# W2 loaded first and stored by rank, three casts ahead of the gelu layer, two low parts on GpSimd

## What is computed

```
ae = layernorm(cond) * ln_g + ln_b            # 2 x 256
h  = gelu(ae @ w1 + b1)                       # 2 x 256
xw = h @ w2 + b2                              # 2 x 4096, w2 is 256 x 4096
x_a, x_b = split(xw);  both reshape(2, 256, RANK=8)
layer = base_layer + einsum('bdr,bkr->bdk', x_a, x_b)
x = x + (x + x @ layer)
h_t = tanh(h_(t-1) @ Wh + x_t @ Wx + b)       # 1024 steps, h_0 = cond
out = x + h_t
```

## Time and profile before

| | us |
|---|---|
| median of 3 runs | 768.34 (767.2 to 768.7) |
| the profiled execution's own time | 767.74 |
| its span, from the first to the last instruction | 764.9 |
| the prologue, up to the first step of the recurrence | 30.25 |
| the recurrence and the last rows | the rest |

### The profile page before, as it was taken

One profiled execution on the slowest core, in us unless ns is written; L12 is line 12 of the kernel. 1 busy time (PEld: TensorE's weight loads), 2 busy tenths in 40 slices (PEclk: granted clock), 3 DMA queues, 4 the chain that ended last, 5 costly groups with the idle time before them and its releaser, 6 DMA issues.

```text
span 764.9 us, 45957 instructions
## 1 busy us (share of the span) xinstructions
PE 689.3 (90%) x18801; PEld 623.6 (82%) x18801; DVE 283.4 (37%) x1539; ACT 497.8 (65%) x5140; POOL 6.4 (1%) x18
## 2 busy tenths in 40 slices
PE   5699999999999999999999999999999999999997
PEld 5588888888888888888888888888888888888886
DVE  6533333333333333333333333333333333333332
ACT  6466666666666666666666666666666666666665
POOL 3000000000000000000000000000000000000000
DMA  8000000000000000000000000000000000000000
GB/s 279 10 6 10 11 11 9 11 7 9 11 11 8 11 8 9 11 11 9 10 7 9 11 11 9 11 7 9 11 11 9 11 8 7 11 11 9 7 7 6
DMA packets 12285, 12.36 MB, mean 16 GB/s; under 512 B 1813, under 2 KB 11056, under 8 KB 12080
## 3 DMA queue, kind: packets, MB, share of 16 engines
q1 hardware_dynamic: 11984, 9.45, 4.3%
q0 software_dynamic: 96, 0.02, 0.0%
HBM read 7.36 MB, written 2.10 MB: 12 GB/s over the span
## 4 chain that ended last, share of the span: by engine, by line
PE 76%; ACT 19%; issue 2%; DMA 1%; SPq 1%; DVE 1%; DVEq 0%; another core or an unknown queue 0%
PE acc L320 49%; ACT h_pre L446 19%; PE pre L320 14%; PE p_w L284 4%; PE pre L300 4%; PE p_w L279 2%; DMA x_in<-x_dram 1%; PE p_w L274 1%; PE pre L297 1%; SPq L218 1%; PE pre L401 0%; SPq L215 0%; DVE lay_s L687 0%; DVE lay_f L683 0%; DVE ab_t L676 0%
## 5 line engine op out<-in xcount | busy, mean ns | idle before, releaser
L320 PE MATMUL acc<-h_pre,wh_s 128*128 128x2 f16 x8192 | 385.5, 168 | 57.8 <-DVE acc L562 0.6
L446 ACT ACTIVATE h_pre<-pre 128x2 f16<-128x2 f32 x2046 | 240.7, 170 | 251.1 <-PE pre L320 251.1
L320 PEld LDWEIGHTS acc<-h_pre,wh_s 128*128 128x128 f16 x8192 | 302.2, 106 | 121.1 <-ACT h_pre L446 105.0
L567 DVE TENSOR_TENSOR h_lo<-p_f,h_pre 128x4 f16<-128x4 f32 x1024 | 165.5, 162 | 461.7 <-ACT p_f L452 457.1
L320 PE MATMUL pre<-h_rnd,wh_s 128*128 128x2 f16 x4092 | 270.2, 170 | 0.0
L320 PE MATMUL acc<-h_lo,wh_s 128*128 128x2 f16 x4096 | 257.5, 167 | 0.0
L320 PEld LDWEIGHTS pre<-h_rnd,wh_s 128*128 128x128 f16 x4092 | 190.7, 108 | 0.1
L320 PEld LDWEIGHTS acc<-h_lo,wh_s 128*128 128x128 f16 x4096 | 189.2, 106 | 0.1
L456 ACT ACTIVATE h_f<-acc 128x4 f32<-128x4 f32 x1024 | 186.4, 182 | 0.5 <-PE acc L320 0.5
L454 ACT ACTIVATE h_rnd<-acc 128x4 f16<-128x4 f32 x1022 | 172.7, 169 | 0.0
L452 ACT ACTIVATE p_f<-acc 128x4 f32<-128x4 f32 x1023 | 161.6, 158 | 0.1
(11 more groups left out here) (76 smaller groups left out, 139.4 us busy)
## 6 DMA issues: line engine op xcount, KB each, us to landing
w_f<-w_dram SPq DMA_DIRECT2D x8, 512.0 KB, 8.4
x_in<-x_dram SPq DMA_DIRECT2D x32, 64.0 KB, 2.3
out_dram<-o_row SPq DMA_DIRECT2D x64, 32.0 KB, 1.9
w_f<-w_dram SPq DMA_DIRECT2D x1, 256.0 KB, 2.8
base_f<-base_dram SPq DMA_DIRECT2D x1, 256.0 KB, 10.8
wh_f<-wh_dram SPq DMA_DIRECT2D x1, 256.0 KB, 10.5
wx_f<-wx_dram SPq DMA_DIRECT2D x1, 256.0 KB, 10.5
cond_r<-cond_dram SPq DMA_DIRECT2D x1, 2.0 KB
```

Of the source, the lines that this page charges most:

```text
L320: return nc.tensor.matmul(dst, wh_s[:, pw, ki, mo * P:(mo + 1) * P], h[:, par, ki, :], start=False, stop=True, skip_group_check=True)
L446: nc.scalar.activation(h_pre[:, n % 2, m, :], src, func, scale=scale).then_inc(s_hpre[(n // HALF) % 2], 1)
L567: nc.vector.tensor_sub(h_lo[:, par].rearrange("p m b -> p (m b)"), p_f[:, 0:COLS], h_pre[:, par].rearrange("p m b -> p (m b)")).then_inc(s ...
```

## The change

**The DMA queues.** SyncE issues piece 0 first, then W1, piece 1, the first block of `x`, pieces 2 to 7, `base`, `wh` and `wx`. The four small loads, `cond` and three vectors, move to ScalarE's queue, ahead of its first instruction.

```diff
-        w2_s = sb("w2_s", [P, 2, NM, 2 * D * RANK], F16)
+        w2_s = sb("w2_s", [P, 2, NM, 4, RANK, P], F16)
+        AHEAD = 3
+        POOLED = [3, 5]
+
+        def by_rank(ap):
+            return ap.rearrange("p (d r) -> p r d", r=RANK)
@@ gpsimd
+            for n in POOLED:
+                q, k = W2_PIECES[n]
+                pool.wait_ge(s_w2hi, n + 1)
+                nc.gpsimd.tensor_sub(w2_s[:, 1, k, q], by_rank(w2_f[:, k, tile_of_ab(q)]),
+                                     w2_s[:, 0, k, q]).then_inc(s_w2pool, 1)
@@ tensor
-            for n, (q, k) in enumerate(W2_PIECES):
+            for n in range(len(W2_PIECES)):
                 if n == 6:
                     turn_x()
...
+                pe.wait_ge(s_w2hi, n + 1)
+                w2_products(n, 0)
+                if n not in POOLED:
+                    pe.wait_ge(s_w2lo, n + 1 - len([m for m in POOLED if m < n]))
+                    last = w2_products(n, 1)
+                for m in POOLED:
+                    if n == m + 2:
+                        pe.wait_ge(s_w2pool, POOLED.index(m) + 1)
+                        last = w2_products(m, 1)
@@ scalar
+            def w2_high(n):
+                q, k = W2_PIECES[n]
+                act.wait_ge(s_w2[n], 16)
+                nc.scalar.copy(w2_s[:, 0, k, q], by_rank(w2_f[:, k, tile_of_ab(q)])).then_inc(s_w2hi, 1)
```

More of the change, by code:

```diff
@@ L140, in cond_recurrence @@
         s_w2lo = sem("s_w2lo")
+        s_w2pool = sem("s_w2pool")
         s_abcol = sem("s_abcol")
@@ L211, in _, with load_w2 @@
         def _(sync):
-            sync.dma_start(cond_r[:, :], cond).then_inc(s_cond, 16)
-            for n, v in enumerate((ln_g, ln_b, b1)):
-                sync.dma_start(vec_r[n * NM:(n + 1) * NM, :], v.rearrange("(m p) -> m p", p=P)).then_inc(s_vec, 16)
+            def load_w2(n):
+                q, k = W2_PIECES[n]
+                sync.dma_start(w2_f[:, k, tile_of_ab(q)], w2[k * P:(k + 1) * P, tile_of_ab(q)]).then_inc(s_w2[n], 16)
+            load_w2(0)
             sync.dma_start(w1_f[:, :, :], w1.rearrange("(k p) n -> p k n", p=P)).then_inc(s_w1, 16)
-            for n, (q, k) in enumerate(W2_PIECES):
-                sync.dma_start(w2_f[:, k, tile_of_ab(q)], w2[k * P:(k + 1) * P, tile_of_ab(q)]).then_inc(s_w2[n], 16)
+            load_w2(1)
+            sync.dma_start(x_in[:, :], x_rows[0:BLOCK]).then_inc(s_xload, 16)
+            for n in range(2, len(W2_PIECES)):
+                load_w2(n)
             sync.dma_start(base_f[:, :, :], base.rearrange("(k p) n -> p k n", p=P)).then_inc(s_base, 16)
-            sync.dma_start(x_in[:, :], x_rows[0:BLOCK]).then_inc(s_xload, 16)
             sync.dma_start(wh_f[:, :, :], wh.rearrange("(k p) n -> p k n", p=P)).then_inc(s_wh, 16)
@@ L392, in _, with w2_products @@
             pe.wait_ge(s_hid, 1)
-            for n, (q, k) in enumerate(W2_PIECES):
+            def w2_products(n, pw):
+                q, k = W2_PIECES[n]
+                for r in range(RANK):
+                    c = 64 + (q * RANK + r) * 2 * NB
+                    product = nc.tensor.matmul(pre[B][:, 0, c:c + 2 * NB], w2_s[:, pw, k, q, r, :],
+                                               hid_s[:, k].rearrange("p s b -> p (s b)"),
+                                               start=n == 0 and pw == 0 and r == 0, stop=True, skip_group_check=True)
+                return product
+            for n in range(len(W2_PIECES)):
                 if n == 6:
                     turn_x()
[L396 to L403, removed]
+                pe.wait_ge(s_w2hi, n + 1)
[7 more added lines that the diff above has]
+                        last = w2_products(m, 1)
             last.then_inc(s_abcol, 1)
@@ L471, in half_block @@
                         act.sem_clear(s_sum[1 - half])
+            act.dma_start(cond_r[:, :], cond).then_inc(s_cond, 16)
+            for n, v in enumerate((ln_g, ln_b, b1)):
+                act.dma_start(vec_r[n * NM:(n + 1) * NM, :], v.rearrange("(m p) -> m p", p=P)).then_inc(s_vec, 16)
             act.wait_ge(s_var, 1)
@@ L476, in _ @@
             nc.scalar.activation(warm[:, :], veps[:, :], ACT.Gelu)
+            def w2_high(n):
+                q, k = W2_PIECES[n]
+                act.wait_ge(s_w2[n], 16)
+                nc.scalar.copy(w2_s[:, 0, k, q], by_rank(w2_f[:, k, tile_of_ab(q)])).then_inc(s_w2hi, 1)
+            for n in range(AHEAD):
+                w2_high(n)
             act.wait_ge(s_hmm, 1)
@@ L488, in high @@
                                      scale=SCALE).then_inc(s_hi, 1)
-            for n, (q, k) in enumerate(W2_PIECES):
-                act.wait_ge(s_w2[n], 16)
-                nc.scalar.copy(w2_s[:, 0, k, tile_of_ab(q)], w2_f[:, k, tile_of_ab(q)]).then_inc(s_w2hi, 1)
+            for n in range(AHEAD, len(W2_PIECES)):
+                w2_high(n)
             high(wh_s, wh_f, s_wh)
@@ L636, in _, with w2_low @@
             last.then_inc(s_ae, 1)
+            def w2_low(n):
+                q, k = W2_PIECES[n]
+                dve.wait_ge(s_w2hi, n + 1)
+                nc.vector.tensor_sub(w2_s[:, 1, k, q], by_rank(w2_f[:, k, tile_of_ab(q)]),
+                                     w2_s[:, 0, k, q]).then_inc(s_w2lo, 1)
+            for n in range(AHEAD):
+                w2_low(n)
             dve.wait_ge(s_hidhi, 1)
             nc.vector.tensor_sub(hid_s[:, :, 1, :], hid[:, :, :], hid_s[:, :, 0, :]).then_inc(s_hid, 1)
[L641 to L650, removed]
+            for n in range(AHEAD, len(W2_PIECES)):
+                if n not in POOLED:
+                    w2_low(n)
             keep_x()
             split_x_high()
-            split_x_low()
             dve.wait_ge(s_b2, 16)
@@ L673, in _, with low @@
             last.then_inc(s_abst, 1)
+            def low(dst, src, n):
+                dve.wait_ge(s_hi, n + 1)
+                nc.vector.scalar_tensor_tensor(
+                    dst[:, 1].rearrange("p k n -> p (k n)"), src[:, :, :].rearrange("p k n -> p (k n)"), SCALE,
+                    dst[:, 0].rearrange("p k n -> p (k n)"), ALU.mult, ALU.subtract).then_inc(s_split, 1)
+            split_x_low()
             low(wh_s, wh_f, 0)
```

## The result

| | before | after |
|---|---|---|
| median | 768.37 us (767.2 to 768.7, 6 runs) | 773.87 us (773.31 to 774.93, 6 runs) |
| span of the profiled execution | 764.9 | 771.4 |
| VectorE's sum of the parts starts | 20.71 | 27.07 |
| first step of the recurrence | 30.25 | 36.61 |

A forecast was written before the change was run, and what follows sets the result against it. Only the recurrence's start could move: earlier loads and slower subtractions put the sum at 19.9 instead of 20.71, less 0.1 us for the new order, so 0.7 us earlier, 767.6 us; range 766.6 to 771.5.

The forecast's parts named there:

- What bounds the kernel: The recurrence has nearly all the time and stays unchanged; only its start, behind VectorE's sum, can move.
- The loads: W2's load stream on SyncE starts 1.30 us earlier; piece 7 lands at 16.05 instead of about 17.15.
- ScalarE's small loads: Four loads issued on ScalarE move its first table load from 0.74 to 2.04, the square root from 2.97 to 3.33.
- The cover: Gelu waits for the cast of piece 2, so up to 3.2 us of lateness on the conditioning path costs nothing.
- The hidden layer: TensorE's first W2 product moves from 9.21 to about 12.6; 128 products then take 4.2 us instead of 7.7.
- The step that failed: ScalarE's cast of W2 with a 32-byte read step was put at 1.05 us, between ends of 1.05 and 1.72.
- the first rival: ScalarE's casts slow too, to 1.72 us; the recurrence starts 2.4 us later, total 770.9 us; chance 0.22.
- The lock: GpSimd's and VectorE's subtractions keep each other out; the recurrence starts 2.7 us later, total 771.0 us; chance 0.18.
- two slow rivals: Slower ScalarE casts, 770.9 us, chance 0.22; GpSimd and VectorE keeping each other out, 771.0 us, chance 0.18.
- GpSimd's price: GpSimd's subtraction of 1024 elements takes at most 2.6 us; slowed by the step to 4.7, total 770.2, chance 0.05.

The follow-up runs named there:

- the step alone: Kernel before with only W2 stored by rank, so casts and subtractions read with a step of 32 bytes: 773.36 us, ratio 1.0073.

## Why the prediction was wrong

**What bounds the kernel** held. All of the difference arose ahead of the sum of the parts, and from the sum on both kernels need the same 9.54 us, where I had added 0.1 us for the new order.

**The loads** were right in kind and uncertain in size. Piece 0 landed at 4.9 (I said 4.7). The last piece landed near 16.2 in the changed kernel, near 15.9 in one run and 17.1 to 17.2 in others of the same order, where I had one figure, 16.05. Alone the part was worth 0.65 us, with an interval that includes no change, because VectorE was on the path. I had read its six low parts before as back to back; they lay (7.70 - 1.225) / 5 = 1.30 us apart, the pace of the loads, where one takes 1.225.

**ScalarE's small loads.** Its issues cost 1.45 us where I had 1.3; the square root ran at 3.73, between my 3.33 and 4.9. That the vectors would land at 5.6 I had missed: I priced the issue and not the transfer among 4 KB packets. The cover that I named, the cast of piece 2, did hide it in the changed kernel; with the loads alone there is no such cover, and it is on the path.

**The hidden layer** came later as I said, at 14.2 instead of 12.6 because the third cast took 2.03 us and the third subtraction 1.99. The loads by rank were as fast as forecast and TensorE kept up.

**The step that failed** is the choice of the cast at the low end, 1.05 us. It took 2.03, even above my upper end of 1.72. I had three rows and drew the wrong thing from each. TensorE's weight load, the only one that read SBUF, I turned into a rate that ScalarE would stay below, 2.1 elements per ns, while a cast whose every element leaves its 16 bytes took ScalarE 1.77 ns per element, more than twice its contiguous 0.82. Its factor of 1.8 I carried as a factor, though the faster engine loses more: 2.2 on ScalarE's slope, 1.7 on VectorE's. And the PSUM row, which holds for PSUM, says nothing of SBUF. The subtraction, put at 1.66 between 1.23 and 2.1, took 1.99. With 2.03 and 1.99 in my own sum for the first rival, the last cast ends near 22.4 and the sum starts near 25.2, which is close to the run without GpSimd (25.73).

**The lock** I held for possible with 0.18 and for the only cause in its case. It is real, and it came on top: 1.3 us from 25.73 to 27.07, and 2.05 us between the last cast and its subtraction. My two slow rivals were priced one at a time, while nothing made them exclude each other; both together lie beyond the range. The range itself left out the upper part of either, and the step alone (773.36) lies beyond it too.

**GpSimd's price** was about right, 2.65 us for the undisturbed piece against at most 2.6, and the step didn't slow it to 4.7. It started at 15.7 and not 12.35. The cast of piece 3 was done only at about 14.4; and GpSimd's load of `b` was used at 7.29 where it had been 5.12, though its queue was as before, and its small work on `b` was then held up by VectorE's subtractions.

## What to carry to other kernels

Before a layout is changed to please one engine's reads, ask which engine now takes the lone elements: in SBUF, leaving the 16 bytes with every element took a cast of 1024 elements from 1.05 to 2.03 us and a subtraction from 1.23 to 1.99, and pairs of float32 were enough to avoid it and still gave TensorE its fast loads. A subtraction moved to GpSimd next to VectorE's of two SBUF inputs is in effect added to VectorE's chain (1.3 to 2 us lost here) rather than run beside it; count both in one sum. And where two unknown costs have different causes, price the case that both come true before the range is closed.

## What the runs showed of the hardware

- A read step of 16, 32 or 64 bytes in SBUF costs about 1.8 ns per element on ScalarE and VectorE alike (2.02 and 1.99 us for 1024); a step of 8 bytes and pairs 32 bytes apart are within 0.07 us of contiguous.
- A float16 write with a step of 16 bytes costs 4.7 us for 1024 elements, more than twice the strided read.
- A read step of 32 bytes in PSUM costs nothing: 0.59 us on ScalarE and 0.69 on VectorE for 512, in order or not.
- TensorE loads 128 float16 weights 4 bytes apart as fast as adjacent ones (16 in 0.51 us), 16 bytes apart in twice the time.
- Two subtractions with two SBUF inputs on VectorE and GpSimd run one after the other (3.19 us for VectorE's 1.22 beside GpSimd's 2.12). Even GpSimd's cast on a single partition waited, 2.07 us for 0.39.
- Small loads on ScalarE's queue were used 2.6 us later when W2's pieces were already under way on SyncE's, and GpSimd's load of `b`, on an unchanged queue, 2.2 us later (7.29 against 5.12).
- The landing of the last of W2's pieces differs by over 1 us between executions with the same queues (last cast at 15.94, 17.10 and 17.22).
